# Macaron block on one NeuronCore: four banks for x's transposes, weight scales behind x's second tile, the second x four slots later, W2's last pieces in the order of the Hadamard pairs

## What is computed

```
def ffn(x):                                   # W1, W3: (2048, 512), W2: (512, 2048)
    hidden = silu(x @ W1.T) * (x @ W3.T)
    hidden = fwht(hidden)                     # Walsh-Hadamard over 2048
    return hidden @ W2.T
x = x + 0.5 * ffn(layernorm(x))
x = x + attn(layernorm(x))                    # ternary weights, 16 heads, chunked linear attention
x = x + 0.5 * ffn(layernorm(x))
```

## Time and profile before

| | |
|---|---|
| median of three executions | 2359.78 us (2358.9 to 2365.25) |
| profiled execution | 2359.46 us |
| its span, first to last instruction | 2357.7 us |
| TensorE matmuls busy | 2336.7 us, 99% of the span |
| VectorE busy | 1223.0 us, 52% |
| ScalarE busy | 717.3 us, 30% |
| GpSimd busy | 149.6 us, 6% |
| mean granted TensorE clock | 0.999 |

### The profile page before, as it was taken

How to read it: one execution, slowest core, us unless ns; L and a number is a source line. 1 busy time by engine, 2 the same in 40 slices (tenths; PEclk the granted TensorE clock), 3 DMA queues, 4 the chain that set the end, 5 groups by cost and what they waited for, 6 DMA issues and landing times.

```text
span 2357.7 us, 31088 instructions
## 1 busy us (share of the span) xinstructions
PE 2336.7 (99%) x12407; PEld 1120.9 (48%) x12407; DVE 1223.0 (52%) x2209; ACT 717.3 (30%) x1228; POOL 149.6 (6%) x126
## 2 busy tenths in 40 slices
PE   8999999999999999999999999999999999999999
PEld 5444444444544454445444544445444544544444
DVE  6677455554565446545554455544564455445312
ACT  6645133223322232233223232333232313332211
POOL 0290000000000000000000000000000000000000
PEclk9999999999999999999999999999999999999999
DMA  9856622331242313322141223421432223131200
GB/s 227 235 142 175 154 81 72 90 86 40 72 90 93 69 28 91 98 83 52 34 142 44 52 79 90 99 54 28 121 68 81 54 54 99 28 90 36 64 27 18
DMA packets 299457, 196.83 MB, mean 83 GB/s; under 512 B 231600, under 2 KB 256176, under 8 KB 295472
## 3 DMA queue, kind: packets, MB, share of 16 engines
q1 hardware_dynamic: 299024, 194.31, 31.6%
q10 hardware_dynamic: 288, 0.52, 0.1%
HBM read 84.68 MB, written 54.53 MB: 59 GB/s over the span
## 4 chain that ended last, share of the span: by engine, by line
PE 93%; DVE 4%; ACT 1%; issue 1%; DMA 1%; POOL 0%; DVEq 0%; SPq 0%; ACTq 0%; POOLq 0%
PE d_bank L1446 27%; PE l_bank L1426 27%; PE g_bank L1426 26%; PE a_bank L1481 5%; PE a_bank L1541 2%; PE a_bank L1464 2%; PE a_bank L1492 1%; PE a_bank L1523 1%; PE a_bank L1528 1%; DVE work L1124 1%; PE a_bank L1506 1%; DVE work L1144 1%; DMA w1t<-kT 0%; ACT work L934 0%; PE a_bank L1530 0%
## 5 line engine op out<-in xcount | busy, mean ns | idle before, releaser
L1446 PE MATMUL d_bank<-w2t,work 128*128 128x512 f16 x2940 | 671.9, 379 | 0.0
L1446 PEld LDWEIGHTS d_bank<-w2t,work 128*128 128x128 f16 x2940 | 284.9, 98 | 332.2
L1124 DVE SCALAR_TENSOR_TENSOR work<-l_bank,l_scale,work 128x512 f32<-128x512 f32 x256 | 191.9, 749 | 443.8 <-PE l_bank L1426 443.8
L1426 PE MATMUL g_bank<-xt,w1t 128*128 128x512 f16 x1536 | 352.4, 379 | 2.2 <-DMA w1t<-kT 2.2
L1426 PE MATMUL l_bank<-xt,w3t 128*128 128x512 f16 x1536 | 352.4, 379 | 0.0
L851 ACT ACTIVATE work<-g_bank,g_scale 128x512 f32<-128x512 f32 x256 | 175.4, 685 | 462.1 <-PE g_bank L1426 460.1
L1426 PE MATMUL l_bank<-work,w3t 128*128 128x512 f16 x1344 | 308.3, 379 | 0.2 <-DVE work L1124 0.2
L1426 PE MATMUL g_bank<-work,w1t 128*128 128x512 f16 x1344 | 308.3, 379 | 0.0
L870 ACT CAST work<-work 128x512 f16<-128x512 f32 x232 | 143.3, 618 | 530.1 <-DVE work L1124 528.3
L1426 PEld LDWEIGHTS g_bank<-xt,w1t 128*128 128x128 f16 x1536 | 147.9, 98 | 175.3 <-DMA w1t<-kT 3.2
L1426 PEld LDWEIGHTS l_bank<-xt,w3t 128*128 128x128 f16 x1536 | 148.1, 98 | 172.8
(11 more groups left out here) (228 smaller groups left out, 1862.0 us busy)
## 6 DMA issues: line engine op xcount, KB each, us to landing
work<-parts_dram SPq DMA_DIRECT2D x192, 128.0 KB, 2.8
x_dram<-work SPq DMA_DIRECT2D x16, 1024.0 KB, 4.1
work<-x_dram SPq DMA_DIRECT2D x11, 1024.0 KB, 7.0
parts_dram<-q_parts SPq DMA_DIRECT2D x32, 256.0 KB, 2.0
parts_dram<-k_parts SPq DMA_DIRECT2D x32, 256.0 KB, 2.2
norm_dram<-cent SPq DMA_DIRECT2D x32, 256.0 KB, 2.0
w2t<-in_L_ffn_W_dram SPq DMA_DIRECT2D x30, 256.0 KB, 3.4
xin<-in_L_attn_x_dram SPq DMA_DIRECT2D x7, 1024.0 KB, 8.5
```

The costliest lines, as they stand in the source:

```text
L1124: nc.vector.scalar_tensor_tensor(out=hfull, in0=l_bank[:], scalar=l_scale[:, j:j + 1], in1=gate, op0=ALU.mult, op1=ALU.mult).then_inc(hful ...
L1426: ins = nc.tensor.matmul(dst[:], wt[:, wp, k, P * j:P * (j + 1)], src[:, xp, k, :], start=(k == 0 and wp == xp), stop=(k == KT - 1 and wp ...
L1446: ins = nc.tensor.matmul(d_bank[t][:], parts[:, hp, P * t:P * (t + 1)], w2t[:, j, wp, :], start=(j == 0 and hp == wp), stop=(j == HT - 1 a ...
```

## The change

Six edits, all in what happens up to the Hadamard pairs.

1. x's four transposes of the first pass get a bank each: `a_bank0`, `a_bank1`, `d_bank2`, `d_bank3`. TensorE no longer waits for a bank there.
2. Chunks 2 and 3 get a scale step of their own. The scale step of chunk 1 stands behind x's second transpose, ahead of the third and fourth; `wprep` 1 stands between these two. Four warm matmuls go. `wsum` 3 and the scales of chunk 3 move behind the first gate tile.
3. The load of the second batch of x goes out behind `wprep` 11 instead of 5, its `rows` steps stand in slots 11, 13, 15 and 17 instead of 7 to 13, and the six parts of its norm in slots 18, 20, ... 28 instead of 14 to 24.
4. W2's pieces take the chunks in the order 0, 2, 1, 3.
5. Their slots: 14, 16, 17, 18, 20, 21, 22, 23, 24, 25, 25, 26, 27, 28, 29, 30.
6. Pair 0 waits for all pieces but the last two; pair 4 waits for these.

```diff
+        turn_bank = a_bank + d_bank[2:4]
...
-        SCALED = [slice(0, 1), slice(1, 2)] + [slice(j, j + 2) for j in range(2, HT, 2)]
+        SCALED = [slice(j, j + 1) for j in range(4)] + [slice(j, j + 2) for j in range(4, HT, 2)]
...
-            steps += [("turn", (key, 0)), ("prep", (key, 3)), ("turn", (key, 1)), ("wprep", 1), ("warm", 4)]
-            steps += [("turn", (key, t)) for t in range(2, TT)] + [("warm", 8), ("wsum", 2), ("wscale", 1), ("wprep", 2), ("wprep", 3)]
-            steps += [("wsum", 3), ("wscale", 2), ("wprep", 4)]
+            steps += [("turn", (key, 0)), ("prep", (key, 3)), ("turn", (key, 1)), ("wscale", 1), ("turn", (key, 2))]
+            steps += [("wprep", 1), ("turn", (key, 3)), ("warm", 8), ("wprep", 2), ("wsum", 2), ("wscale", 2), ("wprep", 3)]
+            steps += [("wprep", 4)]
...
-                add(own, 7 + 2 * t, [("rows", (("ffn1", 1), t))])
+                add(own, 11 + 2 * t, [("rows", (("ffn1", 1), t))])
             for i, part in enumerate(norm_steps(("ffn1", 1))):
-                add(own, 14 + 2 * i, part)
+                add(own, 18 + 2 * i, part)
...
+                if j == 0:
+                    steps += [("wsum", 3), ("wscale", 3)]
...
-                    steps += [("wscale", (j + 5) // 2)]
+                    steps += [("wscale", (j + 7) // 2)]
...
-            splits = (14, 16, 18, 20, 21, 22, 23, 24, 25, 25, 26, 26, 27, 27, 28, 28)
+            splits = (14, 16, 17, 18, 20, 21, 22, 23, 24, 25, 25, 26, 27, 28, 29, 30)
...
+        CHUNK_ORDER = (0, 2, 1, 3)
...
-                    if arg == 5:
+                    if arg == 11:
                         sp.dma_start(x_next, x[1].rearrange("(t p) d -> p t d", p=P)).then_inc(x_next_loaded, 16)
...
-                    t, q = divmod(arg, CHUNKS)
+                    t, q = arg // CHUNKS, CHUNK_ORDER[arg % CHUNKS]
...
-                            pe.wait_ge(w2_turned[b], 16 * KT * CHUNKS // 4)
+                            pe.wait_ge(w2_turned[b], 16 * (KT if b < 2 else KT - 1))
...
+                        if i == 4:
+
+                            for b in (2, 3):
+                                pe.wait_ge(w2_turned[b], 16 * KT)
...
-                    b = take(step, arg)
+                    b, _ = filled(step, arg)
...
-                        ins = nc.tensor.transpose(a_bank[b][:, P * k:P * (k + 1)], cent[:, t % 3, P * k:P * (k + 1)], ident[:])
+                        ins = nc.tensor.transpose(turn_bank[t][:, P * k:P * (k + 1)], cent[:, t % 3, P * k:P * (k + 1)], ident[:])
```

More of the change, by code:

```diff
@@ L884, in _ @@
                     nc.scalar.copy(xt[:, 0, :, P * t:P * (t + 1)],
-                                   a_bank[b][:].rearrange("p (k t) -> p k t", k=KT)).then_inc(a_free[b], 1)
+                                   turn_bank[t][:].rearrange("p (k t) -> p k t", k=KT)).then_inc(a_free[b], 1)
                 elif step == "q":
@@ L1262, in _ @@
                     dve.wait_ge(a_free[b], copied(step, arg, b) + 1)
-                    nc.vector.tensor_tensor(dst[:, 1], a_bank[b][:].rearrange("p (k t) -> p k t", k=KT), dst[:, 0],
+                    nc.vector.tensor_tensor(dst[:, 1], turn_bank[t][:].rearrange("p (k t) -> p k t", k=KT), dst[:, 0],
                                             ALU.subtract).then_inc(a_free[b], 1)
```

## The result

The changed kernel takes 2368.17 us (median of ten executions, 2367.28 to 2369.14). The kernel before, run beside it ten times, takes 2360.76 us (2358.9 to 2367.34). The two medians are 7.41 us, 0.31%, apart. The ratio, reckoned over all twenty executions and not from the two medians, is 1.0024, with a 95% interval of 1.0016 to 1.0032. So the change is slower, by about the 0.3% that counts here as a difference and not clearly more. The ratios of the experiments are reckoned in the same way. The forecast was 2365.7 us and "within 0.3%".

The account below looks back on a forecast made before the run. TensorE's matmuls were taken as the bound, filling 2336.7 of 2357.7 us. Terms -1.5 (first pass), +11.0 (wait), +2.0 (clock), -5.3 (tail) sum to +6.2 on 2359.46, giving 2365.7 us; range 2357.5 to 2370.

Parts of the forecast that it names:

- within 0.3%: Whole kernel: no change that can be told, between 2352.7 and 2366.9 us; chance 0.59.
- First gate tile 17.3 (+0.7): Start, first pass: a scale step ahead of two of x's subtractions moves this tile from 16.58 to 17.3 us.
- Second gate tile 22.8 (+0.1): First pass: its transpose goes out at 18.8 and lands 3.94 later, so the tile starts 0.1 us later.
- Fourth gate tile without its wait, seventh 0 to 0.2: First pass: loading x later removes the fourth's 1.55 us wait; the seventh waits 0 to 0.2, taken as 0.
- Second pass due 100.5: End of first pass: if nothing else waits, the second pass could start at 100.5 us, 1.5 before 101.98.
- Transposes land at 111.5, wait 11.0, start 111.5: Second pass's first gate tile: x's last two transposes queue behind W2's and the row loads; TensorE waits 11.0 us.
- the third rival: Second pass's start: SP can't hand over the transposes; landing 113.2, wait 12.7, time 2367.4 us; chance 0.20.
- The first rival: Second pass's start: the transposes overtake W2's loads; landing 103.4, wait 2.9, time 2355.6 us; chance 0.10.
- Clock +2.0: Behind the second pass's wait: some 4 us at half speed, costing 2.2 at most, taken as 2.0 us.
- Tail -5.3: End of second pass: moved W2 pieces remove the stall behind VectorE's product; pairs start at 186.21 on the old scale.
- so the lag that starts tile 13 late (0.34) stays: Near second pass's end: slots 20 to 24 hold one piece each as before, slot 25 two, so the 0.34 us lag remains.
- From the pairs on unchanged: From the Hadamard pairs on: the order of work is the old one and shifts unchanged.

Follow-up runs that it names:

- e1: The change with W2's eight loads and the four row loads issued behind x's last transpose: 2359.72 us, ratio 0.9993.
- e3: The change with the second x's load, sums and norm back at their old places: 2357.16 us, ratio 0.998.
- e9: The kernel before with the new start (four banks, earlier scales), but W3's first tile ahead of weight tile 1's scale: 2359.46 us, ratio 0.9993.
- e11: The change with only the four row loads behind x's last transpose, all W2 loads still in front: 2366.71 us, ratio 1.0026.
- e8: The kernel before plus late x, new W2 pieces, W2 and row loads behind x's last transpose, and later qkv sums: 2355.69 us, ratio 0.9975.
- e5: The kernel before with only the second x's load, row and norm steps moved later: 2371.32 us, ratio 1.0043.
- e10: The change with W3's first tile ahead of the scale, W2 and row loads behind x's last transpose, and later qkv sums: 2355.44 us, ratio 0.9973.
- e2: The change with four of W2's eight loads kept ahead of x's last two transposes, the other loads behind: 2361.23 us, ratio 0.9997.
- e4: The change with 40 warm matmuls on TensorE ahead of its wait for the second x: 2366.87 us, ratio 1.0018.
- e6: The kernel before with only W2's new piece order and slots and the later wait at pair 4: 2357.27 us, ratio 0.998.
- e7: The kernel before with only the new start (four banks, earlier scales of W1 and W3): 2359.21 us, ratio 0.9988.

## Why the prediction was right, point by point

- **First gate tile 17.3 (+0.7).** 18.02 in the profile, because the clock was at 0.50 from 12 to 18 us. In e1, e3, e9 and e11 it is 16.99 to 17.01, so the order costs 0.4 of the forecast +0.7, and the other 1.0 is a clock that single executions lose (e3 has the same steps there and a clock of 1.00).
- **Second gate tile 22.8 (+0.1).** 23.80, wrong by 1.0. The step "the second gate tile starts at 22.8" looked at that tile's own transpose alone, which did go out at 18.84, where 18.8 was forecast. What I left out is the linear tile between, although I had its transpose 1.5 later: W3's first tile stands behind the same scale step, so its transpose was issued at 16.32 instead of 14.93, and landed 4.8 later, not 3.1. The first linear tile slipped to 21.20 and the second gate tile could not come before 21.20 + 2.6. e9 takes that cause away (19.60).
- **Fourth gate tile without its wait, seventh 0 to 0.2.** Right: 34.16 with none, and the seventh none either; the eighth, at 55.05, is 0.17 over its due time. The seventh's is luck in part: with the old start the same late load costs it 0.84 (e8) and 0.85 (e5), and with the new one nothing (the change and e10); I had not weighed the two against each other.
- **Second pass due 100.5.** 101.68, late by the 1.0 of the start and the 0.17.
- **Transposes land at 111.5, wait 11.0, start 111.5.** The landing was 111.4 and the start 111.50; the wait was 9.82, since due was later. That the number is this close is luck. I had SP hand both transposes over at once, to wait in the DMA engines' rings behind the loads. What the row shows is nearer to the third rival: SP itself was held for 9.56 us and let go at 109.47, 1.9 before the landing. I priced that rival from "held until s_row is in at 109.0", plus 2.7 and 1.5; in fact the issue of the first ended at 106.36, before s_row landed (99.42 + 10.4 = 109.8), and the second was being issued while the first was on its way. What is right in it is the cause, the wait behind W2's bytes, which e1, e2 and e11 show. How much of the wait is SP's being held and how much the busy DMA engines is not separated by any run. The first rival did not happen in any run with all of W2 in front: there the first transpose landed 10.6 to 11.9 us after its issue (the change, e4, e5, e11). The Trainium skill, "DMA: Bandwidth & Descriptors", section "Queues, rings and completion order", lets a small later transfer, on one of the DMA engines, complete before an earlier one has finished on the others, but has each engine's count towards completion land only after all earlier writes of that engine. So it gives no ground for a transfer over all the engines to overtake, and I had taken too much from it; how many engines a transpose uses no row shows.
- **Clock +2.0.** 1.41 here, 2.4 in e5 and 2.5 in e11 (109.75 to 114.83). The size was fair. In the change the granted clock was 0.50 from 111.5 to 113.5, 0.55 in the microsecond behind and 1.00 from 114.5, so the stretch at half speed was shorter than the 4 us I took as a bound. Of the wait at 187 us in before I had said that the first microsecond behind it ran at the full level; its granted clock, 187.2 to 188.2, is 0.84.
- **Tail -5.3.** -3.9. The mechanism is right and shown by e6: no wait at tile 15, none at pair 4. The step that was mis-sized is "so the lag that starts tile 13 late (0.34) stays". I had looked at slots 20 to 25 alone, while pieces 2 and 3 moved to slots 17 and 18, one and two earlier. The waits for VectorE before linear tiles 10, 12 and 13 are 0.17, 0.30 and 0.89 now, and up to tile 13 after is 2.72 late (185.56 against 111.50 + 1.41 + 27 x 2.59 = 182.84) where before was 1.35 (173.26 against 171.91): 1.37 given back, by the earlier pieces as far as is known.
- **From the pairs on unchanged.** True of the order. +1.6 of clock behind the idle of 2.17 us at 1407 fell into this execution.

Forecast +6.2, measured +7.0 at the pairs and +8.6 in the span. The errors: due time +1.2 and wait -1.2, which cancel since the landing sets the start; clock -0.6; tail +1.4; that is 6.2 + 0.8 = 7.0. The rest is the later clock. So the forecast of the time owes its closeness in part to luck: the late start and the shorter wait cancel by the way they hang together, but the smaller gain at the tail and the smaller loss of clock offset each other by chance. The time lies inside the range of 2357.5 to 2370. "Within 0.3%" is a close call: it holds for the ratio (1.0024), and the medians are 7.41 us apart where 7.1 was the bound.

## What to carry to other kernels

A step moved later in a shared list also moves on the DMA queue: look at what it now stands behind there, and whether that waits for anything. Here two transposes of one row tile each landed behind 4 MB of loads that could as well go later, and that one wait took more than the other edits gained. With the big loads issued behind them, the qkv sums later and W3's first tile ahead of the scales, the same schedule gives the fastest kernel measured here. And when a queue is reordered, list what now comes late in turn, down to the engine that waits in order: e1 only moved the stall from TensorE's gate tile to a sum on VectorE, and the repair needed both.

## What the runs showed of the hardware

- A DMA transpose issued behind loads that are still under way holds the issuing queue: 6.45 and 3.06 us for the two issues in the change behind 4 MB and the row loads, 6.12 and 3.98 behind the 4 MB (e11), 2.16 and 5.58 behind 2 MB (e2), 1.34 and 1.23 with W2 behind them (e1). Everything behind them on SP waits as well. Plain loads in the same place were issued in 0.99 us for two (before), and landed late without holding SP.
- The clock behind a short idle is not the same from one execution to the next. The idle of 2.16 to 2.17 us near 1400 us stands in all 13 profiles; nine go on with a gate tile of 2.75 us and four (the change, e4, e5, e8) with one of 3.93 to 4.44. A wait of 3.04 us (e2) left the clock up, one of 2.56 us (e4) did not. Such a tile costs up to 1.7 us. That fits the scatter of before's runs over 2359 to 2368, but whether it is the cause was not tested.
- The same at the start. Before the first of x's transposes, at 11.06, TensorE sat idle for 1.17 to 2.14 us in nine of the profiles, and their granted clock from 12 to 18 us is 1.00. In the other four the idle was 2.22 to 2.58 us and the clock 0.50 (the change) or 0.72 to 0.73 (e7, e10, e11). The length of that idle is set by how soon the warm matmuls ahead of it end, 1.83 + 6.76 = 8.6 in the change, and differs between kernels that are alike there. Only in the change did it move the first gate tile; in e7, e10 and e11 that tile starts at 17.00 to 17.05 as in the rest with the new start.
